# Rotated queries left unscaled: the softmax's exponential takes the inverse norms as its scale and bias

## The chip, the core and the metric

The kernel runs as one program on one core of a Trainium2 chip. The metric is device time in microseconds for the whole program. The text names the engines as the profile does: PE is TensorE (matmuls, and PEld its weight loads), DVE is VectorE, ACT is ScalarE, POOL is GpSimd, SP is SyncE (here it only issues DMAs).

## What is computed

The whole program is eight residual layers over `x` of shape [8, 512, 256]. The change touches one of them, the local layer (`L2_ffn`), which is itself two blocks in a row. In each block the attention half is, cut to what matters:

```python
q, k, v = split(shift_token(x) @ wqkv)            # 8 heads of 64
q = (q / max(norm(q), 1e-12)) * q_scale           # norm over the 64 of a head
k = (k / max(norm(k), 1e-12)) * k_scale
q, k = rotary_xpos(q, k)                          # q*cos*s + rotate_half(q)*sin*s ; k with 1/s
sim = (8 * q) @ k.T                               # windows of 128, looking back one window
sim = where(mask, -big, sim)
attn = softmax(sim)
x = x + (attn @ v) @ wo
```

Rotation is linear, so the inverse norm of a query (one number for each token and head) can be multiplied in before the scores or after them. In the scores' tile a query is a partition, so that there the inverse norm is one number per partition.

## The kernel before, in words

The program is a chain of phases with a barrier between them. In each of the two blocks of the local layer there is a rotary phase (`rotary_qkv`, tiles named `a_...`), an attention phase (`windowed_attention`, tiles named `t_...`) and a gated MLP, which the change does not touch. Order on each engine is written out by hand: every engine has a `step` function, a loop calls it once for each unit, and `at(i)` is the unit that lies i units ahead, so that each step does a part of several units. Semaphores join the engines.

**Rotary phase.** 8 batches of 512 tokens, 4 tiles of 128 tokens each. A unit is one tile of queries (even units) or of keys (odd units), 128 tokens x 512 columns (8 heads x 64): 8 units to a batch, 64 in the phase. The work of a unit n is:
- PE projects it (`project`, L2692, six matmuls into `a_qps`); ACT copies it to SBUF (`a_qsb`, L2753) and squares it (`a_sq`, L2762);
- DVE multiplies it with the cosine table (`a_straight`, L2897) and sums the squares (`a_ss`, L2906); POOL multiplies with the sine table in two halves (`a_crossed`, L2806, two instructions for a unit);
- one step later DVE adds the two (`turned`, L2875). Once for a tile, five small DVE instructions of 16 columns and a square root on ACT make the inverse norms of its 8 query and 8 key heads (L2847, L2852, L2857, L2862, L2867; L2758 on ACT) in `a_rn`;
- in each odd step DVE multiplies two units with their inverse norms (`scaled`, L2885, into `a_rot`), a query unit and a key unit. PE turns each with four transposes (L2715, `a_tps`), which wait for this product, ACT copies the result (L2771, `a_out`), and SP stores it.

Two consecutive steps, one of queries and one of keys, are called a pair here. There are 32 pairs in the loop and one more ahead of it.

**Attention phase.** A unit is two heads x two tiles of 128 queries: 8 units to a batch, 64 in the phase. The program has seven units in flight. Each tile of a head has 256 scores in a row (128 for the first tile of a batch). A unit's work:
- PE makes the scores (L3504, `t_sps`, 12 matmuls);
- DVE adds the mask and takes the extreme of each row in one instruction (`least`, L3625, four for a unit; each has a short read of the accumulator behind it). The score's sign is turned in this kernel (the query's table carries -1), so that the extreme is a minimum;
- ACT takes the exponential (`exponentials`, L3573, four for a unit), with scale -1.0 as an immediate and the row's extreme as bias, a pointer to one number per partition, and sums each row (an accumulator read follows);
- DVE takes the reciprocal of the sums (L3633) and multiplies (`normed`, L3640, four);
- PE transposes (L3515, `t_tps`), ACT copies (L3583, `t_expT`), PE multiplies with the values (L3531), and for every second unit ACT and DVE split the result in two parts (L3589 on ACT, L3646 on DVE) for the output projection (L3545).

ACT's step is, in this order: the split's copy L3589 (every second unit), exponentials of a unit's first tile, copy of the first tile of the unit one older, exponentials of the second tile, copy of the second tile. DVE's step is: reciprocal, the split's subtraction (every second unit), `normed`, `least` of a unit two ahead. POOL loads queries and keys and splits them in two parts (L3464 and L3468, two instructions each for every second unit).

`eng.nop` in `alone` is a way to wait for several semaphores: the first wait sits on the no-operation.

## Time and profile before

| | us |
|---|---|
| runs of the kernel before | 6245.49, 6249.43, 6275.58 (median 6249.43) |
| the profiled execution, first to last instruction (span) | 6247.0 |
| PE busy in the span | 4641.5 (74%) |
| DVE busy in the span | 3907.9 (63%) |
| ACT busy in the span | 2867.3 (46%) |
| POOL busy in the span | 2042.9 (33%) |

The profiled execution is known by its span alone, 2.4 us under the median of the runs. The shares are means over some thirty phases with different limits, and the phases that the change touches are about a fifth of the span: the rotary phases run from about 3328 to 3593 us and from 4212 to 4480 us of the span, the attention phases from about 3599 to 3960 us and from 4488 to 4850 us. The profile is therefore read inside these stretches.

### The profile page before, as it was taken

To read this page: it belongs to the slowest core of one execution; us is meant where nothing else is said; L and a number is where in the kernel's file an instruction comes from. 1 tells how busy PE (TensorE), PEld (TensorE's weight loads), DVE (VectorE), ACT (ScalarE), POOL (GpSimd) and SP (SyncE) were. 2 spreads that over 40 slices of the span, in tenths; PEclk is the share of its full clock that TensorE was granted. 3 is DMA by queue.
4 is the path that set the end of the run, shared out by engine and by line. 5 is a ranking of instruction groups with operands and counts; after the bars stand their busy time and mean duration, and the time that the engine had idled before them with its cause. 6 is when DMAs were issued, how large, how long until landed. Compare 5 with 4: busy or idle time off the path is not lost. (4 is left out here: it accounts for less than half of the span.)

```text
span 6247.0 us, 101680 instructions
## 1 busy us (share of the span) xinstructions
PE 4641.5 (74%) x24902; PEld 2868.6 (46%) x24902; DVE 3907.9 (63%) x8145; ACT 2867.3 (46%) x6151; POOL 2042.9 (33%) x3122
## 2 busy tenths in 40 slices
PE   7455666493879973998676767797677887995897
PEld 4113333342643331885234645686555663333433
DVE  6344555538547875443678956558866556886565
ACT  2235655215227753223564556435456323773353
POOL 0113443000036630221443554124542214542342
PEclk9558989696988986999778989998889998997897
DMA  4999986100063321111551232002321115332533
GB/s 158 283 360 190 211 197 157 45 0 0 0 201 89 97 63 45 43 43 41 155 144 62 102 115 65 27 13 92 129 73 41 28 49 182 92 85 82 179 117 100
DMA packets 317791, 648.30 MB, mean 104 GB/s; under 512 B 73170, under 2 KB 128115, under 8 KB 317384
## 3 DMA queue, kind: packets, MB, share of 16 engines
q1 hardware_dynamic: 245912, 450.68, 22.7%
q0 software_dynamic: 71488, 193.32, 13.1%
q8 instruction: 134, 2.20, 0.1%
q14 instruction: 257, 2.11, 0.1%
HBM read 373.99 MB, written 238.70 MB: 98 GB/s over the span
## 5 line engine op out<-in xcount | busy, mean ns | idle before, releaser
L1115 DVE TENSOR_REDUCE t_nmax<-t_aps 128x2 f32<-128x1024 f32 x700 | 838.0, 1221 | 278.2 <-PE t_aps L1037 272.6
L1222 ACT ACTIVATE t_expT<-t_bps 128x512 f32<-128x512 f32 x1290 | 700.9, 599 | 284.4 <-PE t_bps L1056 235.4
L1056 PE MATMUL t_bps<-t_Q,t_K 51*128 51x512 f32 (+2 forms) x1290 | 525.9, 468 | 60.8 <-ACT t_expT L1222 43.8
L1037 PE MATMUL t_aps<-t_K,t_Q 49*128 49x512 f32 (+2 forms) x1400 | 464.7, 460 | 64.7 <-DMA t_K<-k_halves 28.9
L1056 PEld LDWEIGHTS t_bps<-t_Q,t_K 51*128 51x128 f32 (+2 forms) x1290 | 228.8, 189 | 528.6 <-ACT t_expT L1222 373.5
L2517 DVE TENSOR_TENSOR f_hl<-f_h,f_hh 128x512 fp32r<-128x512 f32 x192 | 203.7, 1061 | 413.3 <-ACT f_hh L2442 413.3
L1083 PE MATMUL t_ops<-t_expT,t_V 128*17 128x512 f32 (+1 forms) x2560 | 414.2, 614 | 0.5 <-ACT t_expT L1222 0.4
L3923 ACT ACTIVATE t_relsb<-t_relsb,t_nmax 128x128 f32<-128x128 f32 (+3 forms) x515 | 277.6, 559 | 272.8 <-DVE t_nmax L3896 264.0
L3857 PE MATMUL t_tps<-ident,t_relsb 128*128 128x128 f32 x1280 | 246.6, 296 | 160.1 <-ACT t_expT L3745 149.3
L2806 POOL TENSOR_TENSOR a_crossed<-a_qsb,a_tab 128x256 f32<-128x256 f32 x272 | 268.1, 1007 | 295.9 <-ACT a_qsb L2753 271.3
L1156 POOL DMA_DIRECT2D t_Q<-q_halves x525 | 270.9, 518 | 143.9 <-POOLq L78 72.9
L3822 POOL TENSOR_TENSOR t_relsb<-t_relsb,t_M 128x128 f32<-128x128 f32 (+1 forms) x384 | 198.5, 546 | 335.5 <-DMA t_relsb<-rel 304.0
L3896 DVE CUSTOM_DVE_ANT_0 t_relsb<-t_sps,t_relsb 128x128 f32<-128x128 f32 (+3 forms) x515 | 234.0, 484 | 83.6 <-PE t_sps L3850 52.6
L3573 ACT ACTIVATE t_prob<-t_summed,t_nmax 128x256 f32<-128x256 f32 (+1 forms) x560 | 265.6, 479 | 26.9 <-DVE t_nmax L3625 22.3
L3857 PEld LDWEIGHTS t_tps<-ident,t_relsb 128*128 128x128 f32 x1280 | 169.0, 150 | 231.4 <-issue 215.7
L1156 POOL DMA_DIRECT2D t_K<-k_halves x525 | 267.5, 512 | 18.6 <-issue 10.3
L3515 PE MATMUL t_tps<-ident,t_prob 128*128 128x128 f32 x964 | 151.7, 303 | 154.4 <-DVE t_prob L3640 154.3
L3583 ACT COPY t_expT<-t_tps 128x512 f32<-128x512 f32 (+1 forms) x276 | 144.3, 523 | 262.6 <-PE t_tps L3515 262.6
L1037 PEld LDWEIGHTS t_aps<-t_K,t_Q 49*128 49x128 f32 (+2 forms) x1400 | 214.5, 199 | 103.8 <-issue 52.4
L1307 PE MATMUL r_o<-r_erk,r_Q 96*128 96x128 bf16 (+3 forms) x512 | 161.0, 460 | 133.2 <-DVEq L1335 92.8
L3745 DVE COPY t_expT<-t_tps 128x128 f32<-128x128 f32 (+1 forms) x256 | 108.0, 422 | 197.9 <-PE t_tps L3857 197.7
L2382 PE MATMUL f_yps<-f_wdh,f_hh 128*128 128x256 f32 x768 | 217.9, 284 | 13.8 <-DVE f_hl L2517 13.8
(441 smaller groups left out, 12543.1 us busy)
## 6 DMA issues: line engine op xcount, KB each, us to landing
rel<-r_out SPq DMA_DIRECT2D x128, 640.0 KB, 5.4
t_relsb<-rel SPq DMA_DIRECT2D x128, 640.0 KB, 5.6
t_Q<-q_halves POOLq DMA_DIRECT2D x420, 64.0 KB, 2.5
t_K<-k_halves POOLq DMA_DIRECT2D x420, 64.0 KB, 2.5
k_halves<-a_parts SPq DMA_DIRECT2D x48, 512.0 KB
q_halves<-a_parts SPq DMA_DIRECT2D x48, 512.0 KB, 5.6
o_xT<-attended SPq DMA_DIRECT2D x32, 512.0 KB, 4.3
f_R<-combine SPq DMA_DIRECT2D x128, 128.0 KB, 3.0
```

Of the source, the lines that this page charges most:

```text
L1037: last = nc.tensor.matmul(aps[:, (t * PPG + i) % 2, x, :], operand(Qr, KA, p, h, slice(t * P, (t + 1) * P)), operand(Kr, KA, p, h, slice(0 ...
L1056: nc.tensor.matmul(bps[:, slot_of(kb, j), :], operand(Kr, KB, p, h, slice(kb * P, (kb + 1) * P)), operand(Qr, KB, p, h, slice(0, S)), star ...
L1083: last = nc.tensor.matmul(ops[j * COL:j * COL + VW, :], V[:, p, kb, g * HG + j, :], expT[:, kb % RING, j, :], start=kb == 0, stop=kb == NT ...
L1115: nc.vector.tensor_reduce(nmax[:, g, t, i * HPT:(i + 1) * HPT], aps[:, (t * PPG + i) % 2], AX.X, ALU.max, negate=True).then_inc(s["maxed"], 1)
L1156: pool.dma_start(dst[o + i * DH:o + (i + 1) * DH, p, cols], rows(src, part, r, g, b)).then_inc(sem, 16)
L1222: nc.scalar.activation(expT[:, kb % RING, j, :], bps[:, slot_of(kb, j), :], ACT.Exp).then_inc(s["expo"], 1 + (PAD if end else 0))
L2382: last = nc.tensor.matmul(o, fast(x), fast(w), start=m == 0 and i == 0 and t % 2 == 0, stop=m == NF - 1 and i == 2, skip_group_check=True)
L2806: last = nc.gpsimd.tensor_tensor(y[:, :, k, :], x[:, :, 1 - k, :], tab[:, 2 * i + 1, t, k * HW:(k + 1) * HW].unsqueeze(1).broadcast_to([P, ...
L3573: nc.scalar.activation(prob[:, u.slot, i, x, 0:w], summed[:, u.slot, i, x, 0:w], ACT.Exp, scale=-1.0, bias=nmax[:, u.slot, i, x:x + 1], ac ...
L3857: last = nc.tensor.transpose(tps[:, u.t % 2, kb * P:(kb + 1) * P], u.tile()[:, kb * P:(kb + 1) * P], G.ident[:, :])
L3896: nc.vector.tensor_tensor_reduce(out=u.tile(), in0=sps[:, u.t, 0:u.w], in1=u.tile(), scale=1.0, scalar=3.0e38, op0=ALU.add, op1=ALU.min, a ...
L3923: nc.scalar.activation(u.tile(), u.tile(), ACT.Exp, scale=-1.0, bias=nmax[:, u.j, u.t:u.t + 1]).then_inc(s["expo"], 1)
```

## The change

In the rotary phase the key units are scaled as before; the query units are not. `straight` has eight slots instead of four (a slot for each unit of a batch), PE transposes the query units straight from it, and `rot` has one slot. The inverse norms go to a tile `rn` that outlives the phase (36 x 16 numbers per partition: 32 tiles and four that are filled with 1.0), whose place is computed from the loop's counter. In the attention phase the query's inverse norm is the scale of each exponential, a pointer instead of the immediate -1.0. The bias must then be the negative maximum times that norm: a new DVE instruction for each unit (`bias`, 128 x 4 numbers) makes it from the maxima in `top`. The first exponential of a unit waits for it instead of each for its own `least`. Signs turn: the table no longer carries -1, the mask is negative, the minimum is a maximum.

```diff
 def rotary_qkv(...)
-        straight = sb("straight", [P, 4, HD])
+        straight = sb("straight", [P, NU, HD])
-        rot = sb("rot", [P, 2, HD])
+        rot = sb("rot", [P, HD])
...
 # PE, step
-                        pe.wait_ge(s["scaled"], n + 1 + 4)
+                        if u % 2:
+                            pe.wait_ge(s["scaled"], b * NT + u // 2 + 1 + NT)
+                        else:
+                            pe.wait_ge(s["rot"], n + 1 + 2)
                         alone(pe)
                         pe.wait_ge(s["turned"], n + 1)
+                        x = rot if u % 2 else straight[:, u, :]
                         for f in range(NT):
-                            last = nc.tensor.transpose(tps[:, u % 2, f * P:(f + 1) * P], rot[:, u % 2, f * P:(f + 1) * P], G.ident[:, :])
+                            last = nc.tensor.transpose(tps[:, u % 2, f * P:(f + 1) * P], x[:, f * P:(f + 1) * P], G.ident[:, :])
...
 # DVE
+                nc.vector.memset(rn[:, TT:TT + NT, :], 1.0)
-                        last = nc.vector.scalar_tensor_tensor(x, x, 1.0 if i else -1.0, sc[:, i, j, :].unsqueeze(1).broadcast_to([P, NT, DH]), ALU.mult, ALU.mult)
+                        last = nc.vector.tensor_tensor(x, x, sc[:, i, j, :].unsqueeze(1).broadcast_to([P, NT, DH]), ALU.mult)
...
-                    dve.wait_ge(s["scaled"], n + 1)
+                    if i:
+                        dve.wait_ge(s["scaled"], b * NT + t + 1)
+                    else:
+                        dve.wait_ge(s["tp"], n + 1)
+                    alone(dve)
...
-                    if i and at(1):
-                        scaled(at(1))
+                    if i and at(2):
                         scaled(at(2))
...
 def windowed_attention(...)
 # ACT, exponentials
+                    if i == 0:
+                        act.wait_ge(s["bias"], u.n + 1)
                     for x in range(2):
-                        act.wait_ge(s["least"], u.n * 4 + i * 2 + x + 1 + 4)
-                        nc.scalar.activation(prob[:, u.slot, i, x, 0:w], summed[:, u.slot, i, x, 0:w], ACT.Exp, scale=-1.0,
+                        h = u.j * 2 + x
+                        nc.scalar.activation(prob[:, u.slot, i, x, 0:w], summed[:, u.slot, i, x, 0:w], ACT.Exp,
+                                             scale=rn[:, ds(u.b * NT + t, 1), h:h + 1].rearrange("p o h -> p (o h)"),
                                              bias=nmax[:, u.slot, i, x:x + 1], accum_out=esum[:, u.slot, i, x:x + 1]).then_inc(s["expo"], 1)
...
 # DVE
-                                                           scale=1.0, scalar=3.0e38, op0=ALU.add, op1=ALU.min,
-                                                           accum_out=nmax[:, u.slot, i, x:x + 1]).then_inc(s["least"], 1)
+                                                           scale=1.0, scalar=-3.0e38, op0=ALU.add, op1=ALU.max,
+                                                           accum_out=top[:, u.slot, i, x:x + 1]).then_inc(s["least"], 1)
+
+                def bias(u):
+                    dve.wait_ge(s["least"], u.n * 4 + 4 + 4)
+                    nc.vector.scalar_tensor_tensor(nmax[:, u.slot], top[:, u.slot], -1.0, rn[:, ds(u.b * NT + u.half * 2, 2), u.j * 2:u.j * 2 + 2],
+                                                   ALU.mult, ALU.mult).then_inc(s["bias"], 1)
...
                 def step(at):
+                    if at(6):
+                        bias(at(6))
                     if at(5):
                         inverse(at(5))
```

On DVE, in the rotary loop, a key step and what follows it, first before, then after (`norms` is the tile `rn`; an ISA row without a tile computes an address in registers):

```order
L2897 TENSOR_TENSOR a_straight<-a_qsb,a_tab 128x512
L2875 TENSOR_TENSOR a_straight<-a_straight,a_crossed 128x512
L2906 TENSOR_REDUCE a_ss<-a_sq 128x8
L2884 REGISTER_ALU
L2885 TENSOR_TENSOR a_rot<-a_straight,a_rn 128x512
L2884 REGISTER_ALU
L2885 TENSOR_TENSOR a_rot<-a_straight,a_rn 128x512
```

```order
L2906 TENSOR_TENSOR a_straight<-a_qsb,a_tab 128x512
L2879 TENSOR_TENSOR a_straight<-a_straight,a_crossed 128x512
L2915 TENSOR_REDUCE a_ss<-a_sq 128x8
L2888 REGISTER_ALU
L2889 ISA
L2889 TENSOR_TENSOR a_rot<-a_straight,norms 128x512
```

One of the two products of 128 x 512 in a pair is gone; everything else keeps its place.

On DVE, in the attention loop, from the last `least` of a step to the reciprocal of the next, before and after:

```order
L3625 ISA t_summed,t_nmax<-t_sps,t_M 128x256
L3625 ISA t_nmax 128x1
L3630 REGISTER_ALU
L3633 RECIPROCAL t_rs<-t_esum 128x4
L3640 TENSOR_SCALAR t_prob<-t_prob,t_rs 128x256 x4
```

```order
L3638 ISA t_summed,t_top<-t_sps,t_M 128x256
L3638 ISA t_top 128x1
L3643 REGISTER_ALU
L3644 ISA
L3644 SCALAR_TENSOR_TENSOR t_nmax<-t_top,norms 128x4
L3648 REGISTER_ALU
L3651 RECIPROCAL t_rs<-t_esum 128x4
L3658 TENSOR_SCALAR t_prob<-t_prob,t_rs 128x256 x4
```

The small product stands ahead of the reciprocal. On ACT the same exponentials stand in the same places, each now with `norms` among its inputs and an address computation ahead of it (second tile of a unit, before and after):

```order
L3572 REGISTER_ALU
L3573 ACTIVATE t_prob,t_esum<-t_summed,t_nmax 128x256
L3572 REGISTER_ALU
L3573 ACTIVATE t_prob,t_esum<-t_summed,t_nmax 128x256
L3581 REGISTER_ALU
L3583 COPY t_expT<-t_tps 128x2x256
```

```order
L3585 ISA
L3585 ACTIVATE t_prob,t_esum<-t_summed,t_nmax,norms 128x256
L3585 ISA
L3585 ACTIVATE t_prob,t_esum<-t_summed,t_nmax,norms 128x256
L3594 REGISTER_ALU
L3596 COPY t_expT<-t_tps 128x2x256
```

Nothing moved there; only the form of the instruction is another.

## Rows read from the trace of the kernel before

**Rows 1.** Busy time of each engine in the rotary and attention loops of both blocks.
```profile
core 0: us, PE busy (x) PEld busy (x) DVE busy (x) ACT busy (x) POOL busy (x), PEclk, DMA share, GB/s
3340.00:3595.00 255.00, 190.41 (x920) 150.46 (x920) 244.10 (x447) 143.27 (x277) 134.32 (x136) 0.95 0.26 98
3625.00:3925.00 300.00, 230.58 (x1934) 172.56 (x1932) 201.67 (x813) 183.15 (x626) 129.19 (x159) 0.91 0.21 64
4225.00:4480.00 255.00, 197.85 (x920) 156.42 (x920) 241.27 (x444) 143.19 (x277) 133.76 (x136) 0.91 0.25 93
4510.00:4845.00 335.00, 260.96 (x2167) 194.46 (x2166) 225.30 (x916) 204.41 (x702) 130.55 (x161) 0.90 0.18 57
```

**Rows 2.** Groups of instructions by line, 3340 to 3595: busy, mean ns, idle before.
```profile
L2875 DVE TENSOR_TENSOR a_straight<-a_straight,a_crossed 128x512 f32<-128x512 f32 x67 | 61.1, 913 | 0.0
...
L2885 DVE TENSOR_TENSOR a_rot<-a_straight,a_rn 128x512 f32<-128x512 f32 x66 | 57.1, 903 | 0.0
...
L2897 DVE TENSOR_TENSOR a_straight<-a_qsb,a_tab 128x512 f32<-128x512 f32 x68 | 48.5, 714 | 5.5 <-ACT a_qsb L2753 5.5
...
L2715 PE MATMUL a_tps<-ident,a_rot 128*128 128x128 f32 x256 | 41.9, 289 | 54.4 <-DVE a_rot L2885 54.4
```

**Rows 3.** The scaled product, both blocks: duration in ns min/median/max.
```profile
L2885 DVE TENSOR_TENSOR a_rot<-a_straight,a_rn x132: 673/828/1218, 3356.3 to 4480.3; 128x512 f32<-128x512 f32 x132
```

**Rows 4.** DVE in order of time, two pairs in parts: start, us, what.
```profile
3445.03 1.97 DVE L2885 TENSOR_TENSOR a_rot<-a_straight,a_rn 128x512 f32<-128x512 f32 x2
3446.92 0.16 DVE L2847 TENSOR_SCALAR a_held<-a_ss 128x16 f32<-128x16 f32 x1
...
3448.98 0.16 DVE L2862 SCALAR_TENSOR_TENSOR a_bend<-a_bend,a_inv 128x16 f32<-128x16 f32 x1
3449.17 0.61 DVE L2867 SCALAR_TENSOR_TENSOR a_rn<-a_bend,a_inv 128x16 f32<-128x16 f32 x1
...
3452.04 1.28 DVE L2885 TENSOR_TENSOR a_rot<-a_straight,a_rn 128x512 f32<-128x512 f32 x2
3453.24 1.21 DVE L2819 TENSOR_TENSOR a_xl<-a_xps,a_xh 128x1024 fp32r<-128x1024 f32 x1
```

**Rows 5.** POOL in order of time, the same stretch.
```profile
3444.59 1.86 POOL L2806 TENSOR_TENSOR a_crossed<-a_qsb,a_tab 128x256 f32<-128x256 f32 x2 [0.63 <-DVE a_straight L2875]
3448.98 1.99 POOL L2806 TENSOR_TENSOR a_crossed<-a_qsb,a_tab 128x256 f32<-128x256 f32 x2 [2.54 <-ACT a_qsb L2753]
```

**Rows 6.** Who waited for whom, 3625 to 3925: us in total, times, longest.
```profile
ACT t_expT L3583 <- PE t_tps L3515: 114.9, 62, 4.0
...
PE t_tps L3515 <- DVE t_prob L3640: 71.4, 50, 4.8
DVE t_rs L3633 <- ACT t_prob L3573: 57.1, 55, 1.7
DVE t_ol L3646 <- ACT t_oh L3589: 24.5, 30, 1.3
```

**Rows 7.** One unit of the attention in order of time.
```profile
3748.15 0.18 DVE L3633 RECIPROCAL t_rs<-t_esum 128x4 f32<-128x4 f32 x1 [1.07 <-ACT t_prob L3573]
3748.36 1.14 DVE L3640 TENSOR_SCALAR t_prob<-t_prob,t_rs 128x256 f32<-128x256 f32 x4
...
3749.74 1.09 PE L3515 MATMUL t_tps<-ident,t_prob 128*128 128x128 f32 x8 [0.73 <-DVE t_prob L3640]
...
3750.43 0.59 ACT L3583 COPY t_expT<-t_tps 128x512 f32<-128x512 f32 x1 [1.13 <-PE t_tps L3515]
...
3750.91 0.51 ACT L3573 ACTIVATE t_prob<-t_summed,t_nmax 128x256 f32<-128x256 f32 x1
...
...
3752.10 0.18 DVE L3633 RECIPROCAL t_rs<-t_esum 128x4 f32<-128x4 f32 x1 [1.23 <-ACT t_prob L3573]
```

**Rows 8.** ACT groups by form, whole program: one pointer operand, then two.
```profile
L3573 ACT ACTIVATE t_prob<-t_summed,t_nmax 128x256 f32<-128x256 f32 x420 | 210.4, 506 | 3.2 <-DVE t_nmax L3625 3.2
...
L1611 ACT ACTIVATE inner<-stream,n_shift,n_rstd 128x256 f32<-128x256 f32 x56 | 27.7, 585 | 47.2 <-POOL n_shift L1604 47.2
```

More of the change, by code:

```diff
@@ L2841, in norms @@
                     t = u // 2
-                    return (b * NT + t, *(x[:, t % 2, :] for x in (ss, held, root, inv, bend, rn)))
+                    return (b * NT + t, *(x[:, t % 2, :] for x in (ss, held, root, inv, bend)), rn[:, ds(b * NT + t, 1), :].rearrange("p o h -> p (o h)"))
                 def limit(at):
@@ L2874, in turned @@
                     dve.wait_ge(s["crossed"], n + 1 + 2)
-                    nc.vector.tensor_tensor(straight[:, u % 4, :], straight[:, u % 4, :], crossed[:, i, :], ALU.add).then_inc(s["rot"], 1)
+                    nc.vector.tensor_tensor(straight[:, u, :], straight[:, u, :], crossed[:, i, :], ALU.add).then_inc(s["rot"], 1)
                 def scaled(at):
@@ L2883, in scaled @@
                     alone(dve)
-                    dve.wait_ge(s["tp"], n + 1)
-                    nc.vector.tensor_tensor(heads(rot[:, i, :]), heads(straight[:, u % 4, :]),
-                                            rn[:, t % 2, i * H:(i + 1) * H].unsqueeze(2).broadcast_to([P, H, DH]), ALU.mult).then_inc(s["scaled"], 1)
+                    dve.wait_ge(s["tp"], n - 1 + NU)
+                    nc.vector.tensor_tensor(heads(rot[:, :]), heads(straight[:, u, :]),
+                                            rn[:, ds(b * NT + t, 1), H:2 * H].rearrange("p o h -> p (o h)").unsqueeze(2).broadcast_to([P, H, DH]),
+                                            ALU.mult).then_inc(s["scaled"], 1)
                 def step(at, following):
@@ L2895, in step @@
                     alone(dve)
-                    dve.wait_ge(s["scaled"], n + 1)
-                    nc.vector.tensor_tensor(heads(straight[:, u % 4, :]), heads(qsb[:, i, :]),
+                    if i:
[3 more added lines that the diff above has]
+                    alone(dve)
+                    nc.vector.tensor_tensor(heads(straight[:, u, :]), heads(qsb[:, i, :]),
                                             tab[:, 2 * i, t, :].unsqueeze(1).broadcast_to([P, H, DH]), ALU.mult).then_inc(s["straight"], 1)
@@ L2914, in step @@
                         lower(following[2], following[0])
-                dve.sem_inc(s["scaled"], 4)
+                dve.sem_inc(s["scaled"], NT)
+                dve.sem_inc(s["tp"], NU - 2)
                 steps(dve, step)
@@ L3367, in _, with windowed_attention @@
                 steps(step)
-def windowed_attention(nc, G, name, qs, ks, vs, wo, onto):
+def windowed_attention(nc, G, name, qs, ks, vs, rn, wo, onto):
     H, DH = 8, 64
@@ L3376, in windowed_attention @@
     lds = " ".join(f"ld{p}{j}" for p in range(2) for j in range(NPAIR))
-    with phase(nc, name, lds + " hi split v0 v1 wo wh wl mask score least expo recip normed turned cp pv upper lower y y_add poolc") as (s, sb, ps):
+    with phase(nc, name, lds + " hi split v0 v1 wo wh wl mask score least bias expo recip normed turned cp pv upper lower y y_add poolc") as (s, sb, ps):
         Q = sb("Q", [P, 2, 2, NPAIR, S])
@@ L3382, in windowed_attention @@
         summed = sb("summed", [P, 2, 2, 2, W])
+        top = sb("top", [P, 2, 2, 2])
         nmax = sb("nmax", [P, 2, 2, 2])
@@ L3611, in _ @@
                 dve.sem_inc(s["y_add"], 2)
[L3612 to L3613 removed]
+                nc.vector.tensor_copy(M[:, 0:P], G.masks[:, 1, :])
+                nc.vector.tensor_copy(M[:, P:W], G.masks[:, 0, :]).then_inc(s["mask"], 1)
                 dve.wait_ge(s["wh"], 1)
@@ L4093, in program @@
         if 5 in STAGES:
-            with nc.sbuf_tensor("inner2", [P, TT, D], F32) as Y:
+            with nc.sbuf_tensor("inner2", [P, TT, D], F32) as Y, nc.sbuf_tensor("norms2", [P, TT + NT, 16], F32) as rn:
                 G.Y = Y
```

11 lines of the change are left out of this document (4 added, 7 removed).

## The prediction

> **What bounds the kernel now.** The busy time of the engines by stretch comes first, since the page's shares are means over phases that the change does not touch. In both rotary loops DVE is busy 244.10 and 241.27 of 255 us, PE 190.41 and 197.85, ACT 143, POOL 134 [rows 1]: DVE sets the pace, and what leaves DVE leaves the time, as long as nothing else takes its place. The next engine is PE at 75 to 78% of the stretch. In the attention loops no engine is full: PE 230.58, DVE 201.67, ACT 183.15 of 300 us [rows 1]. There one must ask who waits for whom. The waits show a ring: DVE waits 55 times, 57.1 us, for ACT's exponentials before the reciprocal; PE 50 times, 71.4 us, for DVE's `normed`; ACT 62 times, 114.9 us, for PE's transposes [rows 6]. The timeline of one unit shows the ring closing: reciprocal at 3748.15, `normed` 3748.36, PE 3749.74, ACT's copy 3750.43, the first of two exponentials 3750.91, next reciprocal 3752.10, 3.95 us later [rows 7]. What makes a link of this ring longer makes the unit longer.
>
> **The change part by part.**
>
> *Term 1, one product of 128x512 less in each pair of the rotary loop.* 132 of these ran, so 66 go [rows 3]. Two prices stand in the trace. Undisturbed, two of them take from 3452.04 to the next start at 3453.24, 1.20 us or 0.60 each; at another pair the two take from 3445.03 to 3446.92, 1.89 us or 0.95 each [rows 4]. The dearer pair has POOL's multiplications beside it (1.86 us from 3444.59), the cheaper one does not: POOL's pair began at 3448.98 and ended by 3450.97 [rows 5]. The mean of the group is 903 ns against a least duration of 673 [rows 2, 3]; less the 0.07 us by which neighbours overlap, that is 0.83 us of DVE's time. The question is who gets the difference of 0.23. POOL issues the same 272 instructions after the change, and DVE's other products of two SBUF tiles suffer too (L2875: mean 913 ns; L2867, 16 columns wide, takes 0.61 us beside POOL where its sister L2862 takes 0.16) [rows 2, 4]. So I expect a collision mostly to move on to the next product, and take 0.65 us, near the undisturbed row: 66 x 0.65 = 42.9 us. Bounds: 66 x 0.83 = 54.8 if the collisions go too; about 20 if every second freed slot is filled by a new collision of 0.6 us (66 x 0.65 less 33 x 0.6 = 23), and a little under it for PE's limits; not a loss, since PE, ACT and POOL each have over 50 us of idle time in the loop [rows 1].
>
> The Trainium skill ("SBUF — State Buffer", section "Who interferes with whom") says that a DVE instruction with two SBUF inputs and a GpSimd instruction that reads SBUF exclude each other, the later one waiting for the whole of the other. The trace agrees: the two products last 1.97 us beside POOL and 1.28 without [rows 4]. By that rule the number of collisions is set by POOL's instructions, which stay, and that speaks for the lower price.
>
> *Waits in the rotary loop.* PE's transposes no longer wait for the scaled product in query units, and for key units it is made at the same place as before, a step ahead of need. PE waited 54.4 us in the first loop for it [rows 2]; this falls, but PE is not the bound, so I count nothing. Some of it comes back through ACT, for whose copies DVE waits 5.5 us [rows 2]: at most 11 us for both blocks, kept for the range. The new DVE waits of `straight` are for a transposition of eight units before and a key product of a batch before, both long past. The computed addresses run in the queue ahead of DVE and have a 0.6 us instruction to hide behind. The memset of 64 columns and the signs cost nothing that shows.
>
> *Term 2, the exponential's scale becomes a pointer.* A 128x256 activation with one pointer takes 506 ns, one with two (scale and bias) 585 ns [rows 8]: +0.08 us; I take 0.085, since the ring sees starts and not means. Of a unit's four exponentials the two of the second tile lie in the ring [rows 7], between ACT's copy and the reciprocal; the two of the first tile run while ACT would wait for PE (1.13 us in that unit, 1.85 in the mean: 114.9/62 [rows 6, 7]). In every second unit the same two also lie ahead of the split (30 waits of DVE for L3589 [rows 6]), on the same chain. So 64 units x 2 blocks x 2 x 0.085 = 21.8 us. Bounds: 0 if the ring has slack that the waits hide, 43.5 if all four count.
>
> The Trainium skill ("ScalarE: Activation LUTs", section "What ACT_TABLE_LOAD costs") gives about 93 ns for each pointer operand of an ACTIVATE; by that figure the term would be an estimated 23.8 us instead of 21.8. It is the rule that speaks against this change.
>
> *Term 3, one more DVE instruction for each unit.* The nearest rows are the reciprocal of the same 128x4 form, 0.18 us, and L2867 beside POOL, 0.61 [rows 4, 7]. It stands where DVE waits for ACT 1.07 and 1.23 us [rows 7], 1.04 in the mean (57.1/55 [rows 6]), and that wait hides it, even when it collides. Its reader, ACT's exponential of the first tile, is not in the ring: ACT has 1.13 us to spare behind it. Behind it in DVE's queue are the reciprocal and `normed`, which need ACT anyway. In the units without that wait (about one in ten) it costs up to 0.25 us: 13 x 0.2, about 2 us. Bounds 0 and 128 x 0.25 = 32 without the cover.
>
> *Term 4, start of the attention.* The first exponential of each block waits for four `least` and the bias instead of one: about 1 us, twice, 2 us.
>
> Sum: -42.9 + 21.8 + 2 + 2 = -17.1 us. Against the span 6247.0 this is 6229.9; the runs' median is 2.4 above the span, and the forecast goes from it: 6249.4 - 17.1 = **6232 us**. About 0.5% (31 us) is what a measurement of this kernel can tell from no change, so this is most likely "the same" by that measure. Its own range: term 1 between 37 and 50, term 2 between 15 and 28, which gives 6213 to 6246.
>
> **The rivals.**
>
> *A. The longer exponentials cost nothing.* The ring might have slack at ACT that the row of waits hides, as long `normed` runs beside POOL show. Against it: DVE's wait is for ACT in 55 units of about 60. Then 6249.4 - 42.9 + 4 = 6210.
>
> *B. Collisions go with the products.* 54.8 us and the 11 us behind ACT's copies: 6249.4 - 65.8 + 25.8 = 6209. For it: mean 903 ns in the rows of exactly these instructions. Against it: POOL's work is the same.
>
> *C. The rotary gain is eaten.* Each freed slot lets DVE reach POOL's result or POOL's instruction sooner, and half is lost: 6249.4 - 20 + 25.8 = 6255. For it: POOL waits for DVE's sum in some pairs (0.63 us [rows 5]), so both run in lockstep.
>
> *D. Slower: the bias is late.* The small product reads two SBUF tiles and stands right where POOL starts its splitting of queries and keys. If it is held, and ACT's first-tile exponential then waits for it, the ring gets a second, longer way: least, bias, exponential, copy. The point from which it decides is the 1.0 us of DVE's wait plus ACT's idle 1.13 us; past this, each tenth of a us in a unit is 12.8 us for the 128 units. From 0.38 us in each unit on, the time is 31 us above the one before; at the 0.5 us of a collision it is 6232 + 64 = 6296. Against it: the rows of waits leave more than that in both places.
>
> **How the numbers follow.** The forecast's case has 0.50, A 0.18, B 0.12, C 0.13, D 0.07. A and B end more than 31 us below the time before, 0.30 together; D alone ends more than 31 us above it, 0.07; the forecast's case and C are within 0.5%, 0.63. The range runs from 6203 to 6258, which takes in A, B and C and leaves out D and the far ends of A and B.
>
> **What would show it.** Rotary loops: L2889 (after) with 66 rows, loops about 21 us shorter each, DVE still busy over 93% there, PE's wait for the product near nothing, mean of the sum L2879 still near 900 ns (collisions moved on) or lower (B). Attention: exponentials of 128x256 at 590 ns; the ring 4.1 us where it was 3.95; DVE's wait for ACT before the reciprocal about as long as before less the bias; phases 10 to 12 us longer each. If the attention phases have not grown, A; if they have grown by over 25 us each and ACT's first-tile exponential waits for DVE, D. The forecast is wrong if the rotary loops give less than 30 us together or the attention takes more than 35.

## The result, and the profile after

| | us |
|---|---|
| changed kernel, median of 8 runs | 6207.83 (6177.67 to 6222.18) |
| kernel before, beside it, median of 8 runs | 6259.88 (6241.31 to 6714.66) |
| ratio | 0.9917, 95% interval 0.9891 to 0.9943 |
| profiled span, before and after | 6247.0 and 6215.5 |

One run of the kernel before, 6714.66 us, was far slower than the others; without it the median is 6257.6.

The change is worth about 52 us (36 to 68 by the interval) where 17 were forecast. The time lies inside the stated range of 6203 to 6258, but that is luck in part: the range had been opened downwards for rivals A and B, the forecast's own 6213 to 6246 misses it, and as a difference (46 less to 9 more than 6249.4) a gain of 52 us lies outside too. "The same" was the wrong side of 0.5%. The phases of the two profiles, in us; a rotary phase is taken from the first load of its table to DVE's first write of the attention's `Wl`, an attention phase from there to the next phase's first load or, in the second block, to the last reciprocal:

| | rotary 1 | rotary 2 | attention 1 | attention 2 |
|---|---|---|---|---|
| before | 274.3 | 279.2 | 360.4 | 355.6 |
| after | 252.4 | 253.1 | 366.8 | 352.5 |
| forecast of the difference | -21 | -21 | +10 to 12 | +10 to 12 |
| measured | -21.9 | -26.1 | +6.4 | -3.1 |
| granted clock of PE, before | 0.92 | 0.89 | 0.89 | 0.88 |
| granted clock of PE, after | 0.95 | 0.95 | 0.90 | 0.92 |

The granted clock is the share of full speed that PE was given, as a mean over the stretch; it has two levels here, 1.0 (2.4 GHz) and 0.5 (1.2 GHz).

The rotary half came as forecast; the attention took 3 us instead of 25. What is left over lies in code that is the same in both: after the last reciprocal of the second attention the changed kernel took 20 us longer in this pair of profiles (1420.5 for 1400.1), which is why the spans differ by 31.5 and the runs by 52. The granted clock in that stretch was 0.87 after and 0.89 before. The last kernel of this text, which has the same change, took 1401.8 us there at 0.89, so these 20 us belong to the execution and not to the change. The experiments below leave that code out.

The busy time by stretch of the changed kernel, the same view as [rows 1]:

```profile
core 0: us, PE busy (x) PEld busy (x) DVE busy (x) ACT busy (x) POOL busy (x), PEclk, DMA share, GB/s
3340.00:3572.00 232.00, 182.28 (x920) 143.47 (x920) 219.79 (x410) 135.83 (x276) 131.13 (x136) 0.98 0.30 109
3600.00:3900.00 300.00, 223.91 (x1895) 169.00 (x1894) 212.61 (x864) 200.75 (x614) 128.49 (x158) 0.91 0.20 64
4205.00:4435.00 230.00, 181.85 (x920) 143.21 (x920) 219.63 (x410) 134.88 (x275) 130.70 (x136) 0.98 0.30 110
4460.00:4795.00 335.00, 249.58 (x2186) 189.75 (x2187) 234.60 (x995) 231.71 (x708) 132.60 (x162) 0.95 0.17 57
```

The same 920 matmuls of a rotary loop now fit in 232 and 230 us instead of 255, with 37 and 34 DVE instructions less, and DVE is still busy 95% of it: DVE still sets the pace. In the attention ACT is busy 200.75 of 300 us where it was 183.15, although it did a little less (614 instructions for 626). The longer exponentials are there; the time they should have cost is not.

Groups by line in the rotary loop (3340 to 3572), and the scaled product over both blocks; columns as in [rows 2] and [rows 3]:

```profile
L2879 DVE TENSOR_TENSOR a_straight<-a_straight,a_crossed 128x512 f32<-128x512 f32 x67 | 61.8, 923 | 0.0
L2906 DVE TENSOR_TENSOR a_straight<-a_qsb,a_tab 128x512 f32<-128x512 f32 x68 | 47.2, 695 | 2.6 <-ACT a_qsb L2756 2.4
...
L2889 DVE TENSOR_TENSOR a_rot<-a_straight,norms 128x512 f32<-128x512 f32 x33 | 29.9, 906 | 0.0
L2718 PE MATMUL a_tps<-ident,a_rot 128*128 128x128 f32 x128 | 20.1, 280 | 39.9 <-DVE a_rot L2889 39.9
...
L2718 PE MATMUL a_tps<-ident,a_straight 128*128 128x128 f32 x128 | 19.2, 272 | 0.0
```

```profile
L2889 DVE TENSOR_TENSOR a_rot<-a_straight,norms x66: 674/830/1259, 3352.8 to 4430.5; 128x512 f32<-128x512 f32 x66
```

Half of the products are gone and each of the others takes what it took (906 ns for 903, the sum 923 for 913): the collisions did move on. The queries' transposes wait for nothing; those of the keys wait 39.9 us of the 54.4 of before, more than the "near nothing" that I forecast. PE is not the bound (182 of 232 us busy), so it does not show in the time.

The exponential by its form, whole program, beside [rows 8], and the new instruction:

```profile
L3585 ACT ACTIVATE t_prob<-t_summed,t_nmax,norms 128x256 f32<-128x256 f32 x420 | 249.2, 598 | 2.9 <-DVE t_nmax L3644 2.9
```

```profile
L3644 DVE SCALAR_TENSOR_TENSOR t_nmax<-t_top,norms x140: 147/164/1524, 3590.5 to 4793.7; 128x4 f32<-128x4 f32 x140
```

598 ns for 506: +92 where 85 were taken. The bias takes 0.16 us in the median; 33 of the 140 take over 0.3 us, the longest 1.52.

The waits in the attention loop, as [rows 6], stretch 3600 to 3900:

```profile
ACT t_expT L3596 <- PE t_tps L3525: 93.9, 59, 4.9
...
PE t_tps L3525 <- DVE t_prob L3658: 76.1, 50, 6.0
DVE t_rs L3651 <- ACT t_prob L3585: 42.4, 47, 1.6
DVE t_ol L3664 <- ACT t_oh L3602: 22.0, 27, 1.1
```

[Rows 6] covers 310 us (3625 to 3935, not to 3925). Over 300 us, 3625 to 3925, the same view of the kernel before has 110.9 us in 59 waits of ACT for PE and 55.8 us in 54 waits of DVE for ACT. So ACT waits 17 us less for PE, and DVE 13 us less for ACT. The first is what longer exponentials do when something else holds the pace. What that is, two timelines show.

### The profile page after: what moved, and what is told of

Read it like the earlier page. It is cut to its first block and busy times, and to the rows that moved or that the text cites. A ratio compares the mean times of both kernels' runs of the same rounds, so it can differ in the third digit from the quotient of the medians.

```text
span 6215.5 us, 102298 instructions
## 1 busy us (share of the span) xinstructions
PE 4619.4 (74%) x24902; PEld 2856.4 (46%) x24902; DVE 3887.0 (63%) x8221; ACT 2909.6 (47%) x6151; POOL 2037.3 (33%) x3122
## 5 line engine op out<-in xcount | busy, mean ns | idle before, releaser
L3943 ACT ACTIVATE t_relsb<-t_relsb,t_nmax 128x128 f32<-128x128 f32 (+3 forms) x515 | 277.9, 559 | 277.2 <-DVE t_nmax L3916 273.8
L2809 POOL TENSOR_TENSOR a_crossed<-a_qsb,a_tab 128x256 f32<-128x256 f32 x272 | 262.3, 985 | 252.4 <-ACT a_qsb L2756 219.5
L3585 ACT ACTIVATE t_prob<-t_summed,t_nmax,norms 128x256 f32<-128x256 f32 (+1 forms) x560 | 317.3, 571 | 34.8 <-DVE t_nmax L3644 34.8
```

Source lines behind the costliest of these rows:

```text
L2809: last = nc.gpsimd.tensor_tensor(y[:, :, k, :], x[:, :, 1 - k, :], tab[:, 2 * i + 1, t, k * HW:(k + 1) * HW].unsqueeze(1).broadcast_to([P, ...
L3585: nc.scalar.activation(prob[:, u.slot, i, x, 0:w], summed[:, u.slot, i, x, 0:w], ACT.Exp, scale=rn[:, ds(u.b * NT + t, 1), h:h + 1].rearra ...
L3943: nc.scalar.activation(u.tile(), u.tile(), ACT.Exp, scale=-1.0, bias=nmax[:, u.j, u.t:u.t + 1]).then_inc(s["expo"], 1)
```

## The second ring

A unit's time is read best from the starts of one instruction, the reciprocal. [Rows 7] is a unit of 3.95 us; I took it as typical. Here is the other unit of the same pair before the change, all engines, directly ahead of it:

```profile
3742.64 1.29 POOL L3468 TENSOR_TENSOR t_Q<-t_Q 128x512 fp32r<-128x512 f32 x1
3742.69 0.18 DVE L3633 RECIPROCAL t_rs<-t_esum 128x4 f32<-128x4 f32 x1 [1.23 <-ACT t_prob L3573]
3743.65 0.69 DVE L3646 TENSOR_TENSOR t_ol<-t_ops,t_oh 128x512 fp32r<-128x512 f32 x1 [0.78 <-ACT t_oh L3589]
3743.89 1.28 POOL L3468 TENSOR_TENSOR t_K<-t_K 128x512 fp32r<-128x512 f32 x1
3744.26 1.72 DVE L3640 TENSOR_SCALAR t_prob<-t_prob,t_rs 128x128 f32<-128x128 f32 x4
...
3746.22 0.87 PE L3515 MATMUL t_tps<-ident,t_prob 128*128 128x128 f32 x6 [1.50 <-DVE t_prob L3640]
...
3748.03 0.98 PE L3504 MATMUL t_sps<-t_K,t_Q 64*128 64x256 f32 x12
...
3749.71 0.56 POOL L3457 DMA_DIRECT2D t_Q<-queries  x1 [4.54 <-PE t_sps L3504]
```

The reciprocals lie 5.46 us apart (3742.69, 3748.15), then 3.95: 9.41 for the pair. After the change, a pair at about the same place:

```profile
3738.10 0.56 POOL L3467 DMA_DIRECT2D t_Q<-queries  x1 [4.53 <-PE t_sps L3514]
...
3740.44 1.29 POOL L3478 TENSOR_TENSOR t_Q<-t_Q 128x512 fp32r<-128x512 f32 x1
3740.87 0.18 DVE L3651 RECIPROCAL t_rs<-t_esum 128x4 f32<-128x4 f32 x1 [0.99 <-ACT t_prob L3585]
3741.70 1.28 POOL L3478 TENSOR_TENSOR t_K<-t_K 128x512 fp32r<-128x512 f32 x1
3741.83 0.69 DVE L3664 TENSOR_TENSOR t_ol<-t_ops,t_oh 128x512 fp32r<-128x512 f32 x1 [0.78 <-ACT t_oh L3602]
3742.44 1.34 DVE L3658 TENSOR_SCALAR t_prob<-t_prob,t_rs 128x128 f32<-128x128 f32 x4
...
3744.02 0.87 PE L3525 MATMUL t_tps<-ident,t_prob 128*128 128x128 f32 x6 [1.30 <-DVE t_prob L3658]
...
3745.83 0.98 PE L3514 MATMUL t_sps<-t_K,t_Q 64*128 64x256 f32 x12
...
3746.14 0.18 DVE L3651 RECIPROCAL t_rs<-t_esum 128x4 f32<-128x4 f32 x1
...
3747.51 0.56 POOL L3467 DMA_DIRECT2D t_Q<-queries  x1 [4.53 <-PE t_sps L3514]
...
3750.28 0.18 DVE L3651 RECIPROCAL t_rs<-t_esum 128x4 f32<-128x4 f32 x1 [1.00 <-ACT t_prob L3585]
```

Now 5.27 and 4.14: the quiet unit is 0.19 longer, just as term 2 has it, and the pair is again 9.41. POOL's loads are 9.41 apart too (3738.10, 3747.51). That is a second ring, as I read it from these rows: PE's scores free POOL's slot (POOL waited 4.53 us for them), POOL issues two loads, casts and subtracts; DVE's `normed` runs beside its subtraction and does not end before it (3745.98 behind 3745.17 before; 3743.78 behind 3742.98 after, 0.80 us in both), PE's transposes wait for `normed`, and the next scores stand behind them in PE's queue. ACT's exponentials are not what these steps wait for last. `normed` was held for 0.38 us less than before (1.34 for 1.72), and the pair kept its length.

Both pairs lie where PE's clock was at its full level. In the kernel before that is not the rule. Here are the pair shown and a later one by the starts of their reciprocals, and `normed` and the transposes of the later pair:

```profile
core 0: us, PE busy (x) PEld busy (x) DVE busy (x) ACT busy (x) POOL busy (x), PEclk, DMA share, GB/s
3742.69:3752.10 9.41, 7.17 (x68) 5.46 (x67) 6.30 (x27) 6.12 (x22) 4.78 (x7) 1.00 0.17 54
3781.08:3791.88 10.80, 8.69 (x68) 6.28 (x67) 7.01 (x28) 6.13 (x22) 4.81 (x7) 0.84 0.17 51
```

```profile
3782.65 2.33 DVE L3640 TENSOR_SCALAR t_prob<-t_prob,t_rs 128x128 f32<-128x128 f32 x4
...
3785.22 1.07 PE L3515 MATMUL t_tps<-ident,t_prob 128*128 128x128 f32 x5 [2.11 <-DVE t_prob L3640]
```

In the long pair `normed` is held for longer (2.33 us for 1.72), PE stands idle for longer ahead of its transposes (2.11 us for 1.50), and PE's clock is at its lower level for a part of the pair. Two phases have 36 pairs with POOL's splitting beside them, if one leaves out the first three of each phase and the edges of the loop, the pair at the turn of each iteration, which takes longer. If a mean under 0.985 counts as below full, the clock was below full in 22 of the 36 in the kernel before, with a median of 10.6 us; in the changed kernel in 8, and the other 28 have a median of 9.42 us. Whether the collision or the clock comes first in a long pair was not tested.

## The experiments

All but the last hold the local layer alone (`STAGES = (5,)`): the other seven layers are left out, so the times are near 1800 us and a few us can be told. Times are medians of 4 runs with lowest and highest. The first four kernels ran on one chip, the next four on a second and the last three of the layer alone on a third; the whole kernel before had 6261, 6257 and 6255 us on the three, within 0.1%, so times are comparable across the chips to some 2 us. Phases are of the profiled execution.

**The layer alone, before and after.**

> Only the local layer of the kernel before is left in the program (its two blocks, constants, load and store); the other seven layers are left out. It is the reference for the runs beside it. All theories expect its phases to last what they last in the whole program: rotary phases about 263 and 279 us, attention phases about 360 and 373 us, so about 1.5 ms in all.

> Only the local layer of the changed kernel. Theory 1 (the rotary phases give about 48 us; the attention's ring is 0.19 us a unit longer, but in units in which DVE waits for POOL's splitting the ring's extra is swallowed by that wait): 40 to 50 us less than s5_before, with both rotary phases 21 to 27 us shorter and both attention phases -3 to +8 us. Rival (the full 22 us of the pointer are there and a chance fast profile hid them): 20 to 27 us less, attention phases +10 to +13 us each.

Measured 1828.45 (1827.52 to 1835.94) and 1775.02 (1769.43 to 1777.09): 53.4 us less. In the order rotary 1, rotary 2, attention 1, attention 2 the phases took 274.8, 274.8, 362.0 and 353.0 before, and 251.7, 251.8, 359.6 and 351.1 after: the rotary 46.1 us less together, the attention 4.3 less, not 25 more. That is a little over the 40 to 50 expected. The whole gain is in this layer, and the 52 us are real. (The 1.5 ms expected of the layer was too low; it has more than these phases.)

**The rotary part alone.** The changed rotary phase with the table's -1, and the old attention; the queries' norm is left out of the scores.

```diff
-    windowed_attention(nc, G, f"t5{d}", q5, k5, vs5, rn, a["L2_ffn_wo"][d], Y)
+    windowed_attention(nc, G, f"t5{d}", q5, k5, vs5, a["L2_ffn_wo"][d], Y)    # the function of before
```

> Only the local layer, with the rotary phase of the changed kernel and the attention phase of the kernel before; the queries' inverse norm is left out. Theory 1: the whole gain is here, 44 to 52 us less than s5_before, attention phases unchanged within 3 us. The rival with a full pointer cost: the same 44 to 52 us here, and s5_after about 22 us above this run; theory 1 has s5_after at most 8 us above it.

Measured 1790.1 (1784.78 to 1792.33), 38.4 less than before. The rotary phases gave 22.3 and 22.8; of the attentions one was 3.6 shorter and one 6.0 longer, though its code is that of before. A phase whose code is the same can thus change by several us. The 38.4 us are under the 44 to 52 that were expected, and the changed kernel came out 15 us below this run, where theory 1 had it up to 8 above.

**The pointer alone.** The kernel before, with the exponential's scale read from a tile filled with -1.0.

```diff
-  summed[:, u.slot, i, x, 0:w], ACT.Exp, scale=-1.0,
+  summed[:, u.slot, i, x, 0:w], ACT.Exp,
+  scale=rn[:, ds(u.b * NT + t, 1), u.j * 2 + x:u.j * 2 + x + 1].rearrange("p o h -> p (o h)"),
```

> Only the local layer of the kernel before, with one edit in the attention phase: the exponential's scale is a pointer (to -1.0, its address computed from the loop's counter) instead of the immediate. Theory 1: exponentials of 128x256 at 590 ns instead of 506, undisturbed units 4.14 and 4.93 us apart instead of 3.95 and 4.74, units beside POOL's splitting with their sum for two unchanged near 9.4 us; 2 to 12 us more in all. Rival (every unit pays): 22 to 24 us more.

Measured 1827.45 (1822.43 to 1830.52): 1.0 us less than before, where term 2 had +21.8. The attention phases were 357.2 and 354.1. The 2 to 12 us more of theory 1 were missed too. This is the term that fell, without bias or rotary change beside it. The nothing is a balance, as the starts of the reciprocals in the two profiles show (sums over both phases, in us):

| | 36 pairs beside POOL | 20 later pairs, POOL done | 6 edges of the loop | first 3 pairs of a phase |
|---|---|---|---|---|
| scale an immediate (layer before) | 364.2 | 177.0 | 73.1 | 65.4 |
| scale a pointer | 345.1 | 185.6 | 79.4 | 65.8 |
| difference | -19.1 | +8.6 | +6.3 | +0.4 |

Where POOL has nothing left to split, the pointer costs its price: 20 pairs at 2 x 0.19 us would be 7.6. (The 6.3 us at the edges are no more than the same code varies: with the immediate they are 73.1 here and 78.9 in the run with the rotary part alone.) Beside POOL it costs nothing: of the pairs at full clock, 28 of 30 last 9.40 to 9.45 us. There the kernel with the pointer is even the faster, because it has fewer long pairs; its clock was below full in 6 of the 36, that of the kernel before in 21. The same holds in every run with POOL's splitting as it was:

| kernel (profiled) | scale | attention, us | granted clock | pairs below full clock, of 36 |
|---|---|---|---|---|
| before, whole program | immediate | 360.4, 355.6 | 0.89, 0.88 | 22 |
| layer before | immediate | 362.0, 353.0 | 0.89, 0.88 | 21 |
| rotary part alone | immediate | 358.4, 359.0 | 0.89, 0.88 | 20 |
| pointer taken away (next) | immediate | 363.5, 352.3 | 0.89, 0.90 | 15 |
| POOL quiet in the rotary phase, before | immediate | 360.7, 353.2 | 0.89, 0.88 | 20 |
| after, whole program | pointer | 366.8, 352.5 | 0.90, 0.92 | 8 |
| layer after | pointer | 359.6, 351.1 | 0.92, 0.94 | 5 |
| pointer alone | pointer | 357.2, 354.1 | 0.93, 0.92 | 6 |
| POOL quiet in the rotary phase, after | pointer | 358.2, 350.2 | 0.92, 0.92 | 4 |

(Alone, the two parts give 38.4 and 1.0, together 53.4. The 14 us that they lack stay open. In the profiled executions they lack 7.6, and 5.4 of these are the rotary phases of the pointer alone, 277.2 and 277.8 us where the same code took 274.8 twice.)

**The pointer taken away from the changed kernel.** Scale 1.0 as an immediate; the norm is left out of the scores, the bias stays.

```diff
-  scale=rn[:, ds(u.b * NT + t, 1), h:h + 1].rearrange("p o h -> p (o h)"),
+  scale=1.0,
```

> Only the local layer of the changed kernel, the exponential's scale again an immediate (1.0, so the queries' inverse norm is left out of the scores and stays in the bias). The small bias product and the new wait remain. Theory 1 (beside POOL's splitting the unit's pair is paced by collisions, and the pointer's 0.19 us only moves DVE past them): quiet pairs fall back to 8.70 us, but pairs beside POOL scatter between 9.4 and 10.9 us as in s5_before; attention phases within 5 us of s5_after. Theory 2 (the bias's placement and the fewer waits gave the attention its gain, the pointer costs its full 11 us a phase): 20 us less in all than s5_after.

Measured 1780.75 (1771.73 to 1782.98), where the changed kernel had 1775.02 on another chip: no gain, the attentions 3.9 and 1.2 us longer than with the pointer. Beside POOL the quicker exponential buys nothing; at full clock the pair's median is 9.41 us here too.

**POOL quiet in the attention.** POOL casts and subtracts 4 columns of queries and keys instead of 512; the loads stay, and most of the split's parts are filled once, so the scores are other numbers.

```diff
-  nc.gpsimd.tensor_copy(fast(x[:, p, 0, j, :]), x[:, p, 1, j, :])
+  nc.gpsimd.tensor_copy(fast(x[:, p, 0, j, 0:4]), x[:, p, 1, j, 0:4])
-  nc.gpsimd.tensor_tensor(fast(x[:, p, 1, j, :]), x[:, p, 1, j, :], x[:, p, 0, j, :], ALU.subtract)
+  nc.gpsimd.tensor_tensor(fast(x[:, p, 1, j, 0:4]), x[:, p, 1, j, 0:4], x[:, p, 0, j, 0:4], ALU.subtract)
```

> Only the local layer of the kernel before; in the attention phases POOL's splitting of queries and keys is cut to 4 columns for each of its instructions (the rest of the high part is filled once, so the scores are other numbers), so POOL hardly reads SBUF beside DVE. All theories: the attention phases get shorter. Theory 1: every pair of units 8.70 us, both phases together 40 us shorter than in s5_before or more.

> The same cut of POOL's splitting in the changed kernel, local layer only. Theory 1 (the pointer lengthens the ring by 0.19 us in each unit and POOL's collisions had hidden that): every pair 9.07 us, attention phases 11 to 13 us longer each than in s5_quiet_before; total gain of the change down to 20 to 28 us where s5_after against s5_before had 53. Rival (the ring is longer only by chance of the profile, or the bias made up for it): the gain stays at 45 to 55 us.

Measured 1764.2 (1762.64 to 1767.72) and 1740.97 (1738.75 to 1744.21). The difference falls from 53.4 to 23.2, and the attention phases grow by 14.8 and 9.5 (328.2 and 324.4 to 343.0 and 333.9): 24.3 us, against 25.8 in terms 2 to 4. The reciprocals on DVE, quiet before and quiet after:

```profile
450.13 0.18 DVE L3638 RECIPROCAL t_rs<-t_esum 128x4 f32<-128x4 f32 x1 [1.23 <-ACT t_prob L3578]
...
454.87 0.18 DVE L3638 RECIPROCAL t_rs<-t_esum 128x4 f32<-128x4 f32 x1 [1.06 <-ACT t_prob L3578]
...
458.83 0.18 DVE L3638 RECIPROCAL t_rs<-t_esum 128x4 f32<-128x4 f32 x1 [1.23 <-ACT t_prob L3578]
```

```profile
453.64 0.18 DVE L3656 RECIPROCAL t_rs<-t_esum 128x4 f32<-128x4 f32 x1 [0.93 <-ACT t_prob L3590]
...
457.80 0.18 DVE L3656 RECIPROCAL t_rs<-t_esum 128x4 f32<-128x4 f32 x1 [1.07 <-ACT t_prob L3590]
```

The quiet unit is 3.96 before and 4.16 after; a pair 8.70 and, by the other starts of the run, 9.07. Away from starts and edges nearly all pairs of both quiet runs are at full clock (33 and 32 of 36), so here the two kernels are compared without the clock. So the forecast's ring and price are right where POOL leaves it alone. With POOL at work both kernels have pairs of 9.41 us at full clock; the old one has many of 10 to 10.8 us besides. In the 56 pairs away from starts and edges the pointer costs 20.5 us, and 56 x 0.37 would be 20.7. (The phases differ, 14.8 and 9.5, mainly at the edges of the loop: 1.6 us more in the first, 1.7 less in the second.)

**POOL placed between DVE's products.** Changed kernel; POOL begins its casts and the keys' subtraction behind two given `normed`.

```diff
+                    if after is not None:
+                        pool.wait_ge(s["normed"], after + 2)
+                        alone(pool)
...
                     for x in (Q, K):
+                        if after is not None and x is K:
+                            pool.wait_ge(s["normed"], after + 3)
+                            alone(pool)
```

> Local layer of the changed kernel with one edit: POOL starts its splitting only after DVE's normed of a unit, and the key's subtraction only after the next unit's normed, so that POOL's instructions fall into DVE's time on PSUM. Theory 1: the collisions with normed go, pairs beside POOL come down from 9.41 to 9.07 us or little above, attention phases 6 to 10 us shorter each than in s5_after, 12 to 20 us in all. If pairs stay at 9.41, what holds them is not a collision of normed with POOL.

Measured 1741.83 (1739.36 to 1743.64): 33.2 less than the changed kernel (on another chip), with all of POOL's work done, and as fast as with POOL quiet on the same chip (1740.97). DVE and POOL of this run, one pair:

```profile
449.18 0.18 DVE L3657 RECIPROCAL t_rs<-t_esum 128x4 f32<-128x4 f32 x1 [0.50 <-ACT t_prob L3591]
...
450.75 1.00 DVE L3664 TENSOR_SCALAR t_prob<-t_prob,t_rs 128x128 f32<-128x128 f32 x4
...
454.10 0.18 DVE L3657 RECIPROCAL t_rs<-t_esum 128x4 f32<-128x4 f32 x1 [0.92 <-ACT t_prob L3591]
454.31 1.14 DVE L3664 TENSOR_SCALAR t_prob<-t_prob,t_rs 128x256 f32<-128x256 f32 x4
...
458.25 0.18 DVE L3657 RECIPROCAL t_rs<-t_esum 128x4 f32<-128x4 f32 x1 [0.47 <-ACT t_prob L3591]
```

```profile
448.74 1.29 POOL L3484 TENSOR_TENSOR t_Q<-t_Q 128x512 fp32r<-128x512 f32 x1
451.89 1.27 POOL L3484 TENSOR_TENSOR t_K<-t_K 128x512 fp32r<-128x512 f32 x1 [1.85 <-DVE t_prob L3664]
```

The pair is 4.92 and 4.15, 9.07: only the first ring is left, and POOL's subtraction of the keys starts 0.14 us behind the end of `normed`. It was expected at 12 to 20 us. The second ring cost more than I thought, and not only in the pairs of 9.41: the edges of the loop came down from 83.2 to 68.5 us in all.

**POOL quiet in the rotary phase.** POOL multiplies one head instead of eight, the rest of `crossed` is filled once, so the rotation is incomplete.

```diff
-  nc.gpsimd.tensor_tensor(y[:, :, k, :], x[:, :, 1 - k, :],
-                          tab[:, 2 * i + 1, t, k * HW:(k + 1) * HW].unsqueeze(1).broadcast_to([P, H, HW]), ALU.mult)
+  nc.gpsimd.tensor_tensor(y[:, 0:1, k, :], x[:, 0:1, 1 - k, :],
+                          tab[:, 2 * i + 1, t, k * HW:(k + 1) * HW].unsqueeze(1).broadcast_to([P, 1, HW]), ALU.mult)
```

> Local layer of the kernel before; in the rotary phases each of POOL's multiplications is cut from eight heads to one (the rest of its result is zero), so POOL reads SBUF beside DVE only briefly. Theory: collisions cost DVE about 1.1 to 1.6 us of a pair's 7.4; the rotary phases get 35 to 50 us shorter each than in s5_before. If POOL does not matter to DVE, under 5 us.

> The same cut in the changed kernel. If the term of one product in a pair is its 0.60 us undisturbed and the rest of the 0.70 us measured in s5_after was collisions, the rotary phases are 19 to 21 us shorter each than in s5_rq_before. If PE (5.1 us of matmuls and transposes in a pair) is the bound once DVE needs less than that, only 8 to 16 us.

Measured 1735.23 (1732.88 to 1736.38) and 1692.59 (1692.07 to 1698.11). The rotary phases go from 230.7 and 228.5 to 211.8 and 211.9, 17.8 us in the mean or 0.54 for each of 33 products; beside POOL it is 23.1 or 0.70. The 19 to 21 us expected were not reached (18.9 and 16.6), and one of the reasons can be PE: in the quiet changed kernel it is busy 180 of 195 us and DVE 177, so DVE is no longer the bound alone. At the 0.60 us of an undisturbed product [rows 4] a phase would have given 19.8. So 3 to 5 us of a phase's 23 are collisions that went with the product. Most of what POOL takes from DVE stays (40 us of a phase, 251.8 to 211.9).

**ACT in another order.** On top of POOL's new place: both exponentials of a step stand ahead of both copies, so that no wait for PE's transposes stands between a unit's exponentials.

```diff
                     for i in range(2):
                         if at(6):
                             exponentials(at(6), i)
+                    for i in range(2):
                         if at(5):
                             copied(at(5), i)
```

> s5_dodge with one more edit: ACT makes all four exponentials of the newer unit before both copies of the older one, instead of taking turns. Theory (the ring normed, transposes, copy, second tile's exponentials, reciprocal sets the 9.07 us of a pair): the exponentials leave the ring, a pair falls to ACT's own work, 7.3 to 8.3 us, and the whole is 45 to 100 us shorter than s5_dodge. Rival (the copies now come later and the ring only has its links in another order): within 10 us of s5_dodge.

Measured 1690.63 (1684.89 to 1691.28), 51.2 less than without it (1741.83, on another chip). The waits from 320 to 600 us, without and with:

```profile
DVE t_rs L3657 <- ACT t_prob L3591: 32.9, 46, 1.1
```

```profile
PE t_tps L3531 <- DVE t_prob L3665: 39.7, 43, 3.9
...
ACT t_prob L3591 <- DVE t_nmax L3651: 25.7, 35, 3.8
```

DVE's wait for ACT before the reciprocal is gone; now PE waits for DVE and ACT for the bias. Most reciprocals come 3.6 to 4.5 us apart, and a pair takes 8.17 us in the median.

**Both in the whole program.** The changed kernel with the last two edits; nothing is left out.

> The whole program: the changed kernel with both edits of s5_reord (POOL's splitting placed behind normed, all exponentials ahead of the copies). The local layer alone gained 1828 - 1691 = 138 us by the three changes together, 84 of it by the two edits beyond the change. Theory (the phases are apart from the rest): 130 to 145 us less than the kernel before, ratio 0.977 to 0.980. If something outside the layer answers to it, the ratio is outside 0.974 to 0.983.

Measured 6109.33 (6103.69 to 6122.11, 5 runs), the kernel before 6248.26 beside it (9 runs): ratio 0.9778, interval 0.9754 to 0.9801. That is 139 us less, and whether it is over 2% the interval leaves open. It beats both kernels, the changed one by about 1.4% (0.9778/0.9917, each against the kernel before on its own chip), and the attention phases are 315.0 and 309.1 us.

## Why the prediction was right and wrong

*Term 1, right.* 42.9 us were forecast; the rotary phases gave 48.0 in the profiled pair and 46.1 in the layer alone, 0.70 us a product for 0.65. (In the profiled pair the second phase of before was 5 us longer than the first, 279.2 for 274.3, with the same code; in the layer alone both took 274.8.) "I expect a collision mostly to move on": mostly, yes (means of 906 and 923 ns kept); of the 0.23 us between an undisturbed product (0.60) and the mean (0.83) a bit under half did go.

*Term 2, the step that failed.* "What makes a link of this ring longer makes the unit longer" was true of one ring, and there were two. The price of the pointer was right (+92 ns), the ring was right (3.95 to 4.14), and its cost shows where POOL has no splitting to do and with POOL quiet. But the time of a pair beside POOL is set by scores, POOL's split, `normed`, transposes: 9.41 us at full clock with and without the pointer. In place, the pointer alone cost -1.0 us for 21.8, and taking it out again gained nothing. That the cost came out at nothing is luck in its size: in the pointer-alone run it did cost 8.6 us in the pairs without POOL and perhaps some at the edges, and the kernel with the immediate lost 19 us in long pairs, most of them below full clock. The forecast had neither.

[Rows 7] shows a quiet unit of 3.95 us. The phase has 69 reciprocals, since the loop runs 64 units and five stand ahead of it; 68 steps of 3.95 would be 269 us, and they take 338. Some of the gap is the longer unit of each pair (4.74 with POOL quiet) and the loop's edge, once an iteration; with POOL quiet the reciprocals take 303 us (302.7, layer alone). The rest, 35 us, went with POOL's work; the granted clock of the phase is also higher there, 0.95 for 0.89. The gap was open to see, and I did not ask what filled it. The count in term 2 was short as well: 70 units have exponentials in each phase, and 70 for 64 would make it 23.8.

*Terms 3 and 4, small as argued.* With POOL quiet, terms 2 to 4 together are 24.3 for 25.8; the bias was not tested by itself. ACT waited 34.8 us in ten waits for it in the whole program, all at the starts of the phases (25.6 us) and the edges of the loop (9.2 us). In between ACT never waited for it, so the case of rival D did not come up there.

*The rivals.* A named the time, 6210 for 6207.8, and the forecast's own test ("if the attention phases have not grown, A") comes out for it. As a difference it falls short, 39 us for 52; the absolute times agree in part because the kernel before took 6259.9 beside it and not 6249.4. The two signs given for a wrong forecast (rotary under 30 us, attention over 35) did not appear, though its mechanism was wrong; neither could tell that. A's reason, slack of the ring "as long `normed` runs beside POOL show", was half of the truth: the longer link is seen in every quiet unit, and it is the wait behind POOL, not slack at ACT, that takes it in. B is right for 3 to 5 us of a phase and wrong for the rest. C and D did not happen. In the sums: term 1 between 37 and 50 and term 2 between 15 and 28 give 6218 to 6244 with the other terms kept, not 6213 to 6246. The Trainium skill's rule of exclusion between DVE and GpSimd ("SBUF — State Buffer", section "Who interferes with whom") was weighed for the rotary phase alone. The same section names `tensor_scalar`, which `normed` is, among the instructions that can contend with GpSimd in a two-port mode. The rows fit this in the attention, where `normed` takes 1.72 or 1.34 us beside POOL and 1.00 without; there it was the one that decided.

*What stays open.* What makes the long pairs of the kernel before: in them `normed` is held for longer and PE's clock is below full for a part, and no run separates the two or shows why the pointer makes them rarer. They are enough to account for the 4 us by which the attention of the layer alone is even shorter after the change. Open too are the 14 us by which the two parts alone fall short of both together.

## What to carry to other kernels

List the starts of one instruction that occurs once a unit, over a whole phase, before pricing a longer link: a unit time that alternates, or that times the units does not give the phase, says that another ring may hold the pace, and a link outside it may cost nothing. Set the granted clock beside each such step, so that units at full clock are compared with units at full clock. Where POOL's work collides with DVE's short products, give it a place by a semaphore: here that was worth 33 us of 1775. A removed instruction on an engine that was 95% busy was worth its undisturbed duration and nearly half of the collision's surplus here (0.70 us, between 0.60 and 0.83).

## What the runs showed of the hardware

- An exponential of 128x256 with a pointer as scale beside a pointer as bias takes 598 ns for 506; the starts of the two in the ring lie 0.60 us apart instead of 0.51.
- A chain of four `normed` of 128x128 takes 1.00 us alone and 1.34 and 1.72 us beside POOL's subtraction in the two pairs at full clock, and it ended 0.80 us behind it in both; in the longer pair shown it takes 2.33. Two engines held together in this way kept a pace of 9.41 us for a pair at full clock, whether the exponentials had the pointer or not.
- Long pairs and the lower clock go together in this attention. With the scale as an immediate 15 to 22 of 36 pairs had a granted clock below full, at a median of 10.6 us; with a pointer 4 to 8.
- At the edge of the attention's loop, once an iteration, a pair takes 10.4 to 15.6 us in every kernel run here where the pairs around it take 8.0 to 9.4 at full clock, nearly always with the clock below full for a part of it.
- An address computed from the loop's counter ahead of each exponential takes 46 ns in ACT's queue and cost nothing that shows: the quiet unit grew by 0.19 us, which the two longer exponentials fill.
